# Two expert stages around a state-space mixer on Trainium2: routing groups of 4, 8, 12, 16 and 24 tiles in stage one, and routing in finer steps

## What is computed

```python
def ffn(x):                                   # E = 8 experts, D = 128, H = 256, two experts per token
    xt = x.reshape(-1, D)
    topk_vals, topk_idx = top_k(xt @ router_w.T, 2)
    g = sigmoid(topk_vals); g = g / (g.sum(-1, keepdims=True) + 1e-10)
    out = zeros_like(xt)
    for e in range(E):
        ge = sum(where(topk_idx == e, g, 0), -1)
        h = silu(xt @ w_gate[e]) * (xt @ w_up[e])
        out = out + ge[:, None] * (h @ w_down[e])
    return out.reshape(x.shape)

x = x + 0.5 * ffn(layernorm(x))
x = x + mixer(layernorm(x))                   # in-projection, causal conv, silu, state scan, gate, rms, out-projection
x = x + 0.5 * ffn(layernorm(x))
```

## Time and profile before

| | us |
|---|---|
| median of 3 executions | 1274.12 (1271.79 to 1275.92) |
| the profiled execution | 1276.78 |
| its span, first to last instruction | 1275.0 |
| granted TensorE clock, mean | 0.93 |
| busy: PE / DVE / ACT / POOL | 1058.2 / 901.3 / 772.7 / 622.3 |

### The profile page before, as it was taken

One profiled execution on the slowest core, in us unless ns is written; L12 is line 12 of the kernel. 1 busy time (PEld: TensorE's weight loads), 2 busy tenths in 40 slices (PEclk: granted clock), 3 DMA queues, 4 the chain that ended last, 5 costly groups with the idle time before them and its releaser, 6 DMA issues. The chain is left out here.

```text
span 1275.0 us, 23744 instructions
## 1 busy us (share of the span) xinstructions
PE 1058.2 (83%) x6351; PEld 887.7 (70%) x6351; DVE 901.3 (71%) x2699; ACT 772.7 (61%) x1987; POOL 622.3 (49%) x879
## 2 busy tenths in 40 slices
PE   3388989999988999998989879896757999999900
PEld 3277877888876777777767667775546888888800
DVE  6578677879634769786868777676865886888832
ACT  5256655556548787778777747866535665555500
POOL 2727567786033333322323225450550378888875
PEclk9989999999989999898989989998687999999955
DMA  8546454454240000000000000010332344444352
GB/s 270 160 128 204 132 169 146 153 173 128 66 158 20 17 18 17 15 15 14 17 13 18 17 14 32 28 34 1 130 134 68 90 117 133 133 134 133 108 159 74
DMA packets 134333, 114.43 MB, mean 90 GB/s; under 512 B 15424, under 2 KB 118336, under 8 KB 134080
## 3 DMA queue, kind: packets, MB, share of 16 engines
q1 hardware_dynamic: 108864, 64.71, 17.0%
q0 software_dynamic: 16384, 33.59, 9.0%
q10 hardware_dynamic: 8960, 14.63, 3.2%
HBM read 52.90 MB, written 59.97 MB: 89 GB/s over the span
## 5 line engine op out<-in xcount | busy, mean ns | idle before, releaser
L622 POOL DMA_INDIRECT x_dispatched<-xn_sb,row x256 | 252.2, 985 | 207.8 <-DVE row L586 111.2
L972 POOL TENSOR_TENSOR x_skip<-tok,d_skip 128x256 f32<-128x256 f32 x64 | 40.9, 638 | 310.2 <-DVE y L1404 183.6
L395 POOL DMA_INDIRECT f_y_in<-y_dispatched,row x160 | 152.5, 953 | 53.1 <-POOL cleared L367 31.7
L1021 PE MATMUL bank<-xT_high,wc_high 128*128 128x512 f32 x256 | 130.2, 509 | 3.1 <-DVE xT_low L1330 3.1
L395 POOL DMA_INDIRECT y_in<-y_dispatched,row x96 | 96.3, 1003 | 37.5 <-issue 18.6
L1021 PE MATMUL bank<-xT_low,wc_high 128*128 128x512 f32 x256 | 104.7, 409 | 0.0
L1021 PE MATMUL bank<-xT_high,wc_low 128*128 128x512 f32 x256 | 104.6, 409 | 0.0
L789 DVE TENSOR_TENSOR f_hf<-f_sg,banks 128x512 f32<-128x512 f32 x84 | 56.4, 671 | 57.5 <-ACT f_sg L763 47.3
L763 ACT ACTIVATE f_sg<-banks 128x512 f32<-128x512 f32 x84 | 49.2, 586 | 77.8 <-PE banks L735 73.8
L763 ACT ACTIVATE e_sg<-banks 128x512 f32<-128x512 f32 x80 | 47.0, 587 | 79.4 <-PE banks L735 79.2
L755 PE MATMUL bank<-shared,f_hh 128*128 x326 | 87.4, 344 | 0.1
(11 more groups left out here) (282 smaller groups left out, 3380.2 us busy)
## 6 DMA issues: line engine op xcount, KB each, us to landing
f_xr<-x_dispatched SPq DMA_DIRECT2D x79, 128.0 KB
y_dispatched<-f_yr SPq DMA_DIRECT2D x79, 128.0 KB
e_xr<-x_dispatched SPq DMA_DIRECT2D x76, 128.0 KB, 2.2
y_dispatched<-e_yr SPq DMA_DIRECT2D x76, 128.0 KB
w_split<-shared ACTq DMA_DIRECT2D x8, 768.0 KB
shared<-w_split SPq DMA_DIRECT2D x8, 768.0 KB, 6.9
x_dispatched<-xn_sb,row POOLq DMA_INDIRECT x256, 2.3
out_dram<-x_sb SPq DMA_DIRECT2D x8, 512.0 KB, 4.1
```

The source lines that it names most:

```text
L395: nc.gpsimd.indirect_dma_start(out=self.y_in[n % 4][k][:], out_offset=None, in_=self.rows[t], in_offset=bass.IndirectOffsetOnAxis(ap=row[k ...
L622: nc.gpsimd.indirect_dma_start(out=xd_dram[g.x_home], in_=xn_sb[:, t, :], in_offset=None, out_offset=bass.IndirectOffsetOnAxis(ap=row[k][: ...
L1021: last = pe.matmul(acc[:], wc[w][:, tap, k * P:(k + 1) * P], xTb[x][:, at:at + 512], start=(tap == 0 and i == 0), stop=(tap == CONV_K - 1 ...
```

## The change

Stage one has groups of 4, 8, 12, 16 and 24 tiles; the pairs are 84 as before, the last group starts at pair 56 instead of 60. Group 2 is normed, turned and multiplied before the pair loop, and only its choice and positions run in steps -3 to 2. The other two start at steps 5 and 17, with their VectorE work in four large steps (`CLOSE`). Scatters of groups 3 and 4 are no longer paced tile by tile; they wait until the group three before them has been read. All x loads and three fills are on SP ahead of the row loads. The mixer's eight weight loads are issued one a step. The sigmoid is done in two parts, one before the pairs and one after the last.

The last stage's first four row loads are issued in the mixer (`FirstRows`), its last four weight loads each as soon as their part of the buffer has been read, and the factors and the addition of the last sequence move to steps -2 and -1 of the last stage (`LastRows`). Its routing starts at steps -1 and 7 instead of 2 and 10; `FIRST_SENT` becomes 6 (was 10), so `ALL_SENT` is 30 (was 34) and tile 0 is gathered at pair 31 (was 34). All three blocks leave out GpSimd's drain at their end. The diff, cut to what is spoken of:

```diff
-X_HOMES = (16, 20, 16, 24)
+X_HOMES = (16, 24, 16, 24)
 Y_HOMES = (8, 16, 16, 16, 24)
-LAYER1 = groups_of((8, 8, 12, 16, 20), (0, 1, 2, 0, 1), (0, 1, 2, 3, 4))
+LAYER1 = groups_of((4, 8, 12, 16, 24), (0, 1, 2, 0, 1), (0, 1, 2, 3, 4))
...
+            def load(self, act, n):
+                to, of = ((self.w_in[:], io["W_in"]), (self.cw[:], io["conv_wT"].partition_broadcast(P)),
...
+                act.dma_start(to, of).then_inc(self.s_in, 16)
...
-            FILLS = [(0, 0, 23), (1, 0, 23), (2, 0, 31), (0, 23, 39), (1, 23, 47), (3, 0, 55), (2, 31, 39)]
+            FILLS = [(0, 0, 15), (1, 0, 23), (2, 0, 31), (0, 15, 39), (1, 23, 55), (3, 0, 55), (2, 31, 39)]
...
+            def sigmoid(self, act, groups):
+                tiles = slice(groups[0].first, groups[-1].end)
+                act.wait_ge(self.s_selb, groups[-1].index + 1)
+                nc.scalar.activation(gate[:, :, tiles], self.best[:, :, tiles], ACT.Sigmoid).then_inc(self.s_gt, 1)
...
+                self.loaded = XB if first_rows else 0
+                self.xr = first_rows.xr if first_rows else [tb(f"xr{i}", [P, 2, D]) for i in range(XB)]
...
             def load(self, sp, i):
+                if i < self.loaded:
+                    return
                 need(sp, self.s_tr, i - XB + 1)
...
+                self.xr = [tb(f"xr{i}", [P, 2, D]) for i in range(XB)]
+                self.s_xr = [sem(f"e2_rows_in{i}") for i in range(XB)]
+
+            def load(self, sp, router):
+                router.wait_sent(sp, self.g.end)
+                for i in range(XB):
+                    rows = xd_dram[self.g.x_home][2 * i * P:2 * (i + 1) * P, :].rearrange("(j p) d -> p j d", p=P)
+                    sp.dma_start(self.xr[i][:], rows).then_inc(self.s_xr[i], 16)
...
+            def factors(self, dve, ch, r):
+
+                rows, route = slice(CT, 2 * CT), slice(0, CT)
+                dve.wait_ge(self.s_q2, CT * BATCH)
+                ch(nc.vector.tensor_scalar(r.var[:, rows], self.ssq[:], 1.0 / INNER, LN_EPS, ALU.mult, ALU.add))
+                ch(nc.vector.tensor_scalar(r.newton[:, rows], self.ssq2[:], 1.0 / D, None, ALU.mult))
+                for j in range(CT):
+                    nc.vector.bn_aggr(r.mv[:, j, :], r.st[:, j, :])
+                ch(nc.vector.scalar_tensor_tensor(out=r.var[:, rows], in0=r.var[:, rows], scalar=LN_EPS, in1=r.newton[:, rows],
+                                                  op0=ALU.mult, op1=ALU.add))
+                ch(nc.vector.tensor_scalar(r.var[:, route], r.mv[:, route, 1], LN_EPS, None, ALU.add))
+                rsqrt(ch, r.rstd[:, 0:2 * CT], r.var[:, 0:2 * CT], r.newton[:, 0:2 * CT])
+                r.shifts(dve, route)
+
+            def finish(self, dve, r):
+
+                dve.wait_ge(norms.s_plus, 2 * BATCH)
+                for c in range(CT):
+                    t = TILES - CT + c
+                    last = nc.vector.scalar_tensor_tensor(out=x_sb[:, t, :], in0=self.ob[:, c, :], scalar=r.rstd[:, CT + c:CT + c + 1],
+                                                          in1=x_sb[:, t, :], op0=ALU.mult, op1=ALU.add)
+                last.then_inc(self.s_x2, 1)
+                dve.wait_ge(self.s_x2, BATCH)
...
-            with nc.Block() as block:
+            with nc.Block(no_gpsimd_drain=True) as block:
...
-                    for half, done in ((0, TILES - CT), (1, TILES)):
-                        sp.wait_ge(s_mid, done)
-                        sp.wait_ge(s_y, done)
-                        for e in range(E // 2 * half, E // 2 * (half + 1)):
-                            sp.dma_start(w_res[:, e, :].bitcast(fp32), w_dram[e * P:(e + 1) * P, :]).then_inc(s_w2, 16)
+                    def weights(e):
+                        sp.dma_start(w_res[:, e, :].bitcast(fp32), w_dram[e * P:(e + 1) * P, :]).then_inc(s_w2, 16)
+
+                    sp.wait_ge(s_mid, TILES - CT)
+                    sp.wait_ge(s_y, TILES - CT)
+                    for e in range(E // 2):
+                        weights(e)
+                    first_rows.load(sp, r)
+
+                    for e, read, count in ((4, s_tk, TILES), (5, s_g, TILES), (6, s_mid, TILES), (7, s_y, TILES)):
+                        sp.wait_ge(read, count)
+                        if e == 6:
+                            sp.wait_ge(s_y, TILES - CT + 2)
+                        weights(e)
...
-                    factors(B)
-                    finish_rows(B - 1)
                     r.chained = rc.n
+                    norms.chained += ch.n
...
+        BEST1, PICK1, BEST2, PICK2, SELECT, COUNT, NEEDS, BASES, ROWS1, ROWS2, TABLE = range(11)
+        CLOSE = (0, 0, 1, 1, 1, 2, 2, 2, 3, 3, 4)
+        EVEN = (0, 0, 1, 1, 2, 3, 3, 3, 4, 5, 5)
+        WIDE = (0, 1, 2, 2, 3, 4, 4, 5, 6, 7, 8)
+        AHEAD_OF_PAIRS = (0, 0, 1, 1, 2, 3, 3, 3, 4, 4, 5)
...
+                self.stages = stages
+                self.bases_read = chosen + stages[BASES]
+                self.rows_known = chosen + stages[ROWS2]
+                self.known = chosen + stages[TABLE]
...
+            def dve(self, dve, c, i):
+                def now(stage):
+                    return i == self.chosen + self.stages[stage]
+
+                places, totals = counts_at(self.g)
+                if now(BEST1):
+                    n = self.g.end - self.part_first
+                    at = R_LG + (self.part_first - self.g.first) * E
+                    self.r.take(dve, self.part_first, n, self.g.first, b_r[:, at:at + n * E], self.taken)
+                    self.r.best_of(dve, c, self.g, 0)
+                if now(PICK1):
+                    self.r.pick(dve, c, self.g, 0)
+                if now(BEST2):
+                    self.r.best_of(dve, c, self.g, 1)
+                if now(PICK2):
+                    self.r.pick(dve, c, self.g, 1)
...
-                self.chosen = start + self.nk
-                self.placed = self.chosen + 2
-                self.known = self.placed + 2
+                super().__init__(r, g, part_first, taken, start + self.nk, stages)
...
-            beside = [Beside(r, g, g.index, g.first, g.index, start) for g, start in zip(LAYER1[2:], (-2, 6, 17))]
-            ex = Experts("e1", tb, LAYER1, r, beside[-1].placed + 1)
-            SIGMOID = beside[-1].known
-            GATES = SIGMOID + 1
+            early = LAYER1[2]
+            fetched_here = [g for g in LAYER1 if g.first < SOON]
+            fetched_later = LAYER1[len(fetched_here):]
+            beside = [Placing(r, early, early.first, early.index, -3, AHEAD_OF_PAIRS)]
+            for g, start, stages in zip(LAYER1[3:], (5, 17), (CLOSE, CLOSE)):
+                beside.append(Beside(r, g, g.index, g.first, g.index, start, stages))
+            ex = Experts("e1", tb, LAYER1, r, beside[-1].bases_read + 1)
...
-            BEHIND = LAYER1[2].first - beside[0].known + 1
-            BACK = TILES - BEHIND
-
-            def released(g, t):
-
-                if g.index < 2:
-                    return -1
-                return beside[0].known + (t - g.first) * 10 // 11 if g.index == 2 else t - BEHIND
+            BACK = PAIRS1 - SOON - 13
+
+            def released(g):
+
+                return LAYER1[g.index - 3].pair_end if g.index >= 3 else -1
             LOADS = 26
-            LATE_X = {-2: 4, -1: 5, 3: 6, 4: 7}
-            STATS = {1: range(-1, 3), 2: range(9, 14)}
-            MOMENTS = {1: 3, 2: 14}
+            STATS = {1: range(0, 4), 2: range(8, 14)}
+            MOMENTS = {1: 4, 2: 14}
...
-            with nc.Block() as block:
+            with nc.Block(no_gpsimd_drain=True) as block:
...
+                    setup.load_x(sp, 4)
+                    setup.load_x(sp, 5)
+                    setup.fill(sp, 2)
+                    setup.load_x(sp, 6)
+                    setup.load_x(sp, 7)
...
-                            r.scatter_paced(pool, ex, g, t, released(g, t))
+                            r.scatter_paced(pool, ex, g, t, released(g))
...
+                    normalise(early)
+                    for i in range(-3, PAIRS1 + 2):
...
-                        if i == SIGMOID:
-                            r.sigmoid(act)
-                        if i in LATE_X:
-                            setup.load_x(act, LATE_X[i])
-                        if i == 0:
-                            setup.fill(act, 2)
-                        if i in (10, 14):
-                            setup.fill(act, 3 if i == 10 else 4)
+                        if i == -1:
+                            r.sigmoid(act, fetched_here)
+                        if i == PAIRS1:
+                            r.sigmoid(act, fetched_later)
+                        if i in (6, 10):
+                            setup.fill(act, 3 if i == 6 else 4)
...
-                        if i == LOADS:
-                            mixer_weights.load(act)
+                        if 0 <= i - LOADS < 8:
+                            mixer_weights.load(act, i - LOADS)
...
-                        if i == GATES:
```

(26 more changed lines are left out.)

200 lines of the change are left out of this document (117 added, 83 removed).

## The result

| | before | after |
|---|---|---|
| median, us (17 runs each) | 1275.88 (1271.79 to 1281.03) | 1270.89 (1267.02 to 1276.97) |
| ratio, 95% interval | | 0.9961 (0.9945 to 0.9977) |
| profiled span, us | 1275.0 | 1269.0 |

A forecast was written before the change was run, and what follows sets the result against it. TensorE was taken as nearly full in stage one's second half, DMA as full in the first 28 us, GpSimd's gathers as setting the end. 5.7 - 16.6 = -10.9 gave 1264.1 span, 1263 us median; range 1246 to 1280.

The forecast's parts named there:

- T(0): T(n) is when VectorE starts pair n's hidden product; for pair 0 forecast at 51.0, 10.3 earlier.
- T(83): VectorE's start of pair 83's hidden product, near stage one's end; forecast at 351.9, 5.4 later.
- Start, steps 0 to 32: Stage one up to pair 32: smaller first group, waits of 7.61 and 3.39 go; pair 32 at 181.3, 11.6 earlier.
- SP's queue: Start of stage one: 4 MB ahead of the first row loads, hidden by weight split and choice, costed at nothing.
- The last group: Stage one: 48 scatters finish late, store 48 stands behind load 56; VectorE waits 16.7 us at pair 50's out rows.
- Cold clock: TensorE after the last group's wait in stage one: granted clock 0.50, costing 2 more.
- The sigmoid at the end: End of stage one: second sigmoid behind the last hidden copy, costing 0.3.
- Change of stage and last stage: From the mixer's end on: drain and row load go, gathers start earlier; the end follows 16.6 earlier.
- no new wait: Rival: the last group of stage one brings no wait, stage one ends 11 early; 1247 us, chance 0.17.
- scatters slower than 1.75 each: Rival: the last group's 48 scatters in stage one take longer than 1.52, at 1.85 1280 us; chance 0.11.
- a late first row: Rival: first rows come behind all 4 MB on SP, land at 56, start gains nothing; 1274 us, chance 0.08.
- a last stage without gain: Rival: barrier held and norm wait eats the rest, only three pairs' earlier gathers left; 1271 us, chance 0.10.

The follow-up runs named there:

- sizes_before: Changed kernel with layer one's groups back at 8, 8, 12, 16 and 20 tiles; 1304.6 us, ratio 0.9968 where the kernel before took 1305.0.
- last_stage_only: Kernel before with only the changed mixer end and last stage, stage one as before; 1295.4 us, ratio 0.9895 where the kernel before took 1305.0.
- last_stage_only_2: Kernel before with only the changed mixer end and last stage, run on another chip; 1260.5 us, ratio 0.9873 where the kernel before took 1276.2.
- the second half alone: Kernel before with only the changed mixer end and last stage, stage one as before; on chip D 1260.5 us, ratio 0.9873.
- after_here: Changed kernel, unaltered, rerun beside its two halves on one chip; 1271.1 us, ratio 0.9965 where the kernel before took 1276.2.
- after_third: Changed kernel, unaltered, rerun as yardstick on another chip; 1308.4 us, ratio 1.0014 where the kernel before took 1306.8.
- after_again: Changed kernel, unaltered, rerun as yardstick on another chip; 1341.2 us, ratio 1.0066 where the kernel before took 1332.5.
- long_memset: Changed kernel with the memset between scatters and layer one's gathers on 384 columns instead of 192; 1314.2 us, ratio 1.0059.
- stores_first: Changed kernel with the stores of pairs 48 to 51 ahead of pair 56's load in SP's queue; 1306.2 us, ratio 0.9992.
- no_memset: Changed kernel without the memset and its wait between scatters of layer one's last group; 1344.9 us, ratio 1.0267.

## Why the prediction was partly right

The terms in the prediction's order, forecast and first trace:

| step | forecast | measured |
|---|---|---|
| T(0) | 51.0 | 50.1 |
| T(32) | 181.3 | 181.4 |
| first scatter of the last group | 185.3 | 186.1 |
| from it to the last one's start | 71.2 | 74.0 |
| from there until VectorE goes on | 5.7 | 5.0 |
| VectorE's wait | 16.7 | 21.0 |
| T(53) | 262.6 | 265.4 |
| T(53) to T(83) | 89.3 | 92.5 |
| T(83) against before | +5.4 | +11.3 |
| end of stage one, further | +0.3 | +1.7 |
| mixer (to its last scatter) | 0 | -1.3 |
| last stage to the last gather | -16.6 | -17.9 |
| sum | -10.9 | -6.2 |

**Start, steps 0 to 32: right**, within 0.9 us. But I gave the start's gain to the wait for late x that goes, and to earlier rows together; sizes_before shows that with 8 tiles in the first group it is nearly all gone (T(0) 59.8, and 60.8 in last_stage_only). And it is right for this chip alone: on B and C T(32) is 201.1 and 186.9.

**SP's queue: right here, for a thinner reason than given.** I hid the 4 MB behind the split and the choice. In the trace the first rows reach TensorE at 43.6, and VectorE, through with its choice, waits 0.45 for them: they come just in time, and with 16 scatters the new order costs about 4.

**The last group: the mechanism was right in place, carrier and releaser, and its size was off.** This is the step that failed: the wait of 16.7 was 21.0, and T(83) came 11.3 later than before's and not 5.4. First, the scatters' pace: 1.52 is the undisturbed interval (47 of them are 71.4, not 71.2); among the 47 there are longer ones, as shown above, 3.16 at 235.7 and 2.0 at 201.2; all together 2.8. Before has the same one (3.17 at 239.1), so it could have been read: the sum should have gone by first to last start of a whole group, not by one interval times the count. This, the start that was 0.8 late and the 0.7 saved behind the last scatter make T(53) 2.8 later. Second, the need time: VectorE came to the waiting place at 265.05 - 21.00 = 244.05, not at 245.5; that makes the wait longer, but not T(53) later. Third, the recovery, which cost 3.2 more than forecast: I took before's 90.1, less 1.83 and 1 for waits without successor, plus 2 for the clock. In the profiles of chip D this stretch is 92.2 to 92.9 with the long wait and 89.8 to 92.2 without, and much of the difference is one step (from pair 70 to 71) that takes 2.8 in some and 4.3 in others, last_stage_only_2 among them. So nothing in them bears out the 2.8 that I took off, and why that step takes longer stays open.

**Cold clock: right in kind.** After the idle time the granted clock is 0.50, its lower level, from 250 to 270, and full behind it; in this group it happens once. By the Trainium skill, "TensorE: Matmul & The Clock Gate", section on HAM oscillation, waits for DMA bring the slow clock back again and again; the trace has one such wait and one such stretch.

**The sigmoid at the end: mis-sized.** 0.3 was for the activation alone. ScalarE takes it, with a table load of 1.28, before the last out low, and the operations of the gates follow on VectorE's path: 1.7.

**Change of stage and last stage: right in the sum**, -17.9 for -16.6, and confirmed by the second half alone (-15.7 on chip D). But the way there was another. Counted from the mixer's last scatter, T(31) is 11.1 earlier and not 6.5, outside its bounds of 3 and 9: 4.3 of it come between T(0) and T(31), 100.3 instead of before's 104.7, where I had 104.3 (on chip D the two are 100.7 and 102.7, so about half of it lies in this one trace of before). The first gather is 20.0 earlier by the same count, not 17.5, and the gathers then take 2.1 longer than before's, not 0.9, so that two misses partly cancel.

Of the rivals, none came: not "no new wait", not scatters slower than 1.75 each (74.0 / 47 = 1.57), not a late first row, not a last stage without gain. That the last one's figure, 1271, is the measured time is chance. The range held the result, also by some luck: stage one's 7.3 too little and the 2.6 too much behind it have opposite signs. The sum missed because its one large uncertain term was taken at the short end.

## What to carry to other kernels

Where one engine's work must be through before another's queue goes on, compare two chains end to end: rows known, count times pace with its hiccups, and the steps until the first use. The sizes of groups should make these meet: 4, 8, 14, 18 and 20 instead of 4, 8, 12, 16 and 24 keeps the early start and takes the wait away: on chip D 0.978 of the time of before and, against the changed kernel, 20.6 us; on B, 1.0019, it is worth much less. A store queued behind a load that can wait hands that wait to everyone who needs its buffer; but moving it ahead can only help if the rows are late (here it shortened the way from the load to T(56) by 2), and costs if they are early.

## What the runs showed of the hardware

**Indirect DMAs issued without room between them hold the other engines.** With 1.26 between scatters ScalarE and VectorE stood up to 22 us for products long made; with 1.35 and a memset of 0.11 on one column up to 14.5; with 1.52 and a memset of 0.27, at most 1.2 on one chip and up to 2 to 3 us at a time on others. The chips' difference shows in where ScalarE's operations start within GpSimd's cycle. If starts were spread evenly, 26% would lie 0.6 to 0.8 and 1.3 to 1.5 us after an issue began. Counted between 120 and 180 us: after 22 of 86, after_here 19 of 88; after_third 39 of 77, after_again 39 of 63; long_memset, beside after_third, about 23 of 86. But it isn't the chip alone: on chip A stores_first has 42 of 77 and sizes_before 45 of 70, while last_stage_only, with the stage one of before, has 23 of 71, as before has 21 of 75 in the first trace. The same 60 us in after_here and after_again (columns as in rows 1):

```profile
120.00:180.00 60.00, 57.81 (x419) 51.47 (x419) 41.12 (x100) 41.79 (x103) 39.55 (x64) 1.00 0.51 157
```

```profile
120.00:180.00 60.00, 49.56 (x273) 41.66 (x274) 28.92 (x70) 31.03 (x77) 39.98 (x64) 0.83 0.30 96
```

GpSimd does the same 64 operations, the others a quarter to a third less. The granted clock falls to 0.83 as a consequence or beside it; that wasn't told apart. Why an engine's wait ends only in parts of GpSimd's cycle stays open, as does why chips differ. By the Trainium skill, "SBUF — State Buffer", section "SBUF: two separate sides", only VectorE shares a port pair with GpSimd, and TensorE and ScalarE never wait for anyone there. ScalarE's wait of 22.00 in no_memset isn't explained by that; the measurement decides.

**Such a chip turns the change's sign**: 1.0066 where the hold is strongest. There T(32) is 201.1, the wait for the last group shrinks to 4.6 since the pairs are late themselves, and yet the total isn't better than before's. The runs on chip A point to the cause: there it is the new stage one whose ScalarE is held from 120 to 180 us, and the one of before isn't. What in it brings the hold on wasn't tried alone; one candidate is that the scatters of groups 3 and 4 are no longer paced by the pairs, tile by tile.
